# A graph convolution on one core: the one-hot matrix becomes the stationary operand, over groups of 512 edges

## The chip, the core and the metric

The kernel runs on one core of a Trainium2 chip. Its engines are TensorE (PE, with its weight loads as PEld), VectorE (DVE), ScalarE (ACT), GpSimd (POOL) and SyncE (SP), each with its own queue of instructions; semaphores tie them together. The metric is the device time of one execution in microseconds (us). Lower is better.

## The reference

12500 nodes with 128 features `x` (32 scalars and 32 vectors of 3), 412500 edges from `src` to `dst`, sorted by `dst`. Each edge has 4 attributes and 8 radial inputs. Cut to what matters:

```python
f0 = x0 @ W1_0e / sqrt(32);  f1 = einsum('nui,uw->nwi', x1, W1_1o) / sqrt(32)
e0, e1 = feat0[edge_src], feat1[edge_src]          # gather: 1 scalar and 3 vector parts, 32 wide
ea0, ea1 = edge_attr[:, :1], edge_attr[:, 1:4]
h = gelu(edge_scalar_attr @ W_mlp1 / sqrt(8));  h = gelu(h @ W_mlp2 / sqrt(64))
w00, w01, w10, w11 = h @ Wp_00, h @ Wp_01, h @ Wp_10, h @ Wp_11
out0_a = w00 * e0 * ea0
out0_b = w11 * sum(e1 * ea1[:, None, :], -1) / sqrt(3)
out1_a = (w01 * e0)[:, :, None] * ea1[:, None, :]
out1_b = w10[:, :, None] * e1 * ea0[:, :, None]
n0, n1 = segment_sum(mid0, edge_dst), segment_sum(mid1, edge_dst)    # mid: the outs, joined
y = cos * self + sin * (n @ W2) / sqrt(64)
x = layernorm(x + y)
```

All numbers are float32, but for the indices.

## The kernel before

`acc` holds the 12500 nodes as columns of 128 features and stays in SBUF. The program has three stages.

The first makes a table of features in HBM, from which edges are gathered later. Twenty-five batches of 4 x 125 nodes are loaded (SP, `load_x`, L274), transposed (PE L564), copied to `acc` (ACT L446), multiplied with `wfeat` (PE L591), copied (DVE L812) and stored by SP in 6 pieces (`store_table`, L287). Beside it DVE reduces the destinations of each group of 256 edges to their smallest number (L803, L804), POOL subtracts it (L383). Then all source indices and offsets are transposed by PE (L578) into `src_all` and `rel_all`, the attributes (L625) into `ea_all`, and the initial sums are made (L604, copied at L799). A flag tells whether all destinations of a group lie within a window of 16 nodes; here this holds for every group, and the `Else` branches don't run.

The second is the loop over 202 blocks of 2048 edges, which are 8 groups of 256. Block 0, the blocks 1 to 200 as 50 rounds of four, and block 201 are written out separately. The last block starts early enough to be full, and its doubled edges are left out. Per block:

- POOL gathers 16 tiles of 128 rows with an indirect DMA each (L388), in four chunks of 4 tiles, into one of 4 slots of `gath`. It waits for the block's indices in `idx` (L407), which ACT copies out of `src_all` (L450) in its step, three blocks ahead.
- SP loads the radial inputs `e8` (L343), one load for each block.
- PE transposes them (L642); ACT copies them (L484); layer 1 is 8 products of 128 columns (L650), ACT applies the activation (L472); layer 2 is 2 products of 512 columns (L656), ACT applies the activation (L478). All this is done for block b+1 in step b.
- `radial` (PE L666): 8 products of 256 columns make the four weights of every edge, in 4 chunks of one PSUM bank each.
- `multiply` (DVE L875, L878): for each chunk, radial weights (PSUM) times gathered rows (SBUF), into `prod`.
- `select` (DVE L862, L867): offsets are compared with 0 to 15 (`sel01`), then the one-hot matrix is multiplied with each of the 4 attributes: `sel`, 128 x 1024 for a block.
- `segment_sum` (PE L682): for each group, `prod` is the stationary operand (128 x 128) and `sel` the moving one (16 or 48 columns), 32 products per block. The result `z_ps` has features as rows.
- ACT copies the sums (`copy_sums`, L488), PE applies the second weights (`convolve`, L691, 4 products), DVE adds 8 windows of 16 columns into `acc` (`add_windows`, L900).

PE's order in a step is written out by hand (`step`, L696): each chunk's `radial`, then a part of the next block's layers, then the segment sum of two chunks earlier. DVE's step takes the four chunks in order, with `select` for the next block ahead of chunk 2, and the windows of the block before at the end. A float32 product shows up as two MATMUL records in the profile.

The third stage transposes the sums back (L763), normalises (DVE L964, L967, ACT L545, L550) and stores (L357).

Of the kernel before, what the change touches and what calls it, by code (L numbers as in the profile page):

```python
# [7 lines left out]
INT32 = mybir.dt.int32  # L8
# [9 lines left out]
NODE_P = 125  # L18
# [11 lines left out]
GROUP = 256  # L30
# [10 lines left out]
WINDOW = 16  # L41
EA_SLOTS = 8
SLOTS = 4
QUADS = (BLOCKS - 2) // SLOTS
assert BLOCKS == 2 + SLOTS * QUADS
# [14 lines left out]
def build_program(nc, x, src, dst, ea4, ea8, W1_0e, W1_1o, W_mlp1, W_mlp2, Wp, W2_0e, W2_1o, out):  # L60
    ctx = ExitStack()
    with ctx:
# [7 lines left out]
        base_dram = nc.dram_tensor("group_bases", [ROWS, 128], INT32, kind="Internal").ap()  # L70


        acc = sb("acc", [128, NODES + WINDOW])
        ea_all = sb("ea_all", [128, ALL_GROUPS * 2 * 4])
        rel_all = sb("rel_all", [128, ALL_GROUPS * 2], BF16)
        src_all = sb("src_all", [128, (BLOCKS + 2) * TILES], INT16)
        gath = sb("gath", [128, SLOTS, TILES, FEAT])
        idx = sb("idx", [128, SLOTS, TILES], INT32)
        e8 = sb("e8", [128, SLOTS, 128])
        e8T = sb("e8T", [128, 128])  # L80
        zsb = sb("zsb", [128, GROUPS * 4 * WINDOW])
        ident = sb("ident", [128, 128])
        iota_i = sb("iota_i", [128, WINDOW], INT32)
        iota_w = sb("iota_w", [128, WINDOW], BF16)
# [3 lines left out]
        wfeat = sb("wfeat", [128, 128])  # L88
        winit = sb("winit", [128, 128])
        conv = sb("conv", [128, 4, 128])  # L90
        base_f = sb("base_f", [128, ROWS])
        relmax = sb("relmax", [128, ROWS + 1])
        base13 = sb("base13", [ROWS, 128], INT32)
        base_row = sb("base_row", [1, ROWS * 128], INT32)
        flag_i = sb("flag_i", [1, 8], INT32)
        stats = sb("stats", [128, 4, NORM, 6])
# [4 lines left out]

        work = sb("work", [128, 9216])
        prod = work[:, 0:4096].rearrange("p (c t f) -> p c t f", c=CHUNKS, t=CT)
        sel = work[:, 4096:6144].rearrange("p (b t k w) -> p b t k w", b=2, t=TILES, k=4)
        h1 = work[:, 6144:7168].rearrange("p (h n) -> p h n", h=2)
        h2 = work[:, 7168:9216].rearrange("p (b e a) -> p b e a", b=2, a=8)
        ea_rows = work[:, 0:EA_SLOTS * 1024].rearrange("p (b e) -> p b e", b=EA_SLOTS)

        dst_rows = work[:, 2048:2048 + ROWS * 256].rearrange("p (c e) -> p c e", c=ROWS)
        src_rows = work[:, 2048 + ROWS * 256:2048 + 2 * ROWS * 256].rearrange("p (c e) -> p c e", c=ROWS)  # L110
        assert 2 * ROWS * 256 + 2048 <= 9216
        wself_raw = zsb[:, 0:128]
        x_rows = ea_all[0:NODE_P, 0:NODE_J * FEAT].rearrange("p (j d) -> p j d", d=FEAT)
        feat_rows = gath[0:NODE_P, :, :, :].rearrange("p s t f -> p (s t) f")[:, 0:PIECE_SLOTS * PIECE, :]\
            .rearrange("p (b j) f -> p b j f", b=PIECE_SLOTS)
        sel01 = sb("sel01", [128, TILES, WINDOW])
        conv_stage = sb("conv_stage", [128, 4, 128])

        diag = work[:, 4096:5120].rearrange("p (t k n) -> p t k n", t=2, k=4)
        gen_z = work[:, 3072:4096].rearrange("p (t k n) -> p t k n", t=2, k=4)  # L120

# [4 lines left out]
        z_ps = bank[6]  # L126
        t_ps = bank[0][:, 0:128]
        y_ps = bank[7][:, 0:128]

# [4 lines left out]
        s_dst = sem("dst_in")  # L134
        s_src0 = sem("first_src_in")
        s_src = sem("src_in")
        s_ea = [sem(f"ea_in{i}") for i in range(EA_SLOTS)]
        s_eaz = sem("ea_tail_zeroed")
# [6 lines left out]
        s_iota = sem("iota_ready")  # L145
        s_prep = sem("vector_chain")
        s_wnode = sem("node_weights_ready")
        s_xt = sem("x_transposed")
# [858 lines left out]
```

## Time and profile before

| | |
|---|---|
| median of 3 timed runs | 4366.4 us (4364.33 to 4367.3) |
| the profiled execution's own span | 6104.2 us |
| PE busy in it | 4593.2 us, 75% |
| PEld busy | 4019.8 us, 66% |
| POOL busy | 3171.7 us, 52% |
| DVE busy | 1755.8 us, 29% |
| ACT busy | 976.0 us, 16% |
| mean granted clock of TensorE | 0.707 |
| DMA | 254.36 MB, 42 GB/s on average |

The profiled execution is a single one, taken by the hardware profiler, and here it is much longer than the timed ones. Busy time counts an engine's own instructions; waiting, branching and issuing by its queue are not in it. PE's products are pipelined and their ends are modelled. The granted clock is a share of 2.4 GHz, and each moment has one of two levels, 1.0 or 0.5; a mean between them is a share of time.

### The profile page before, as it was taken

The page shows a single profiled execution, that of the slowest core. Times are in us where ns is not written, and L with a number is a line of the kernel's source. Part 1 is how long each engine was busy: PE and PEld are TensorE (multiplying, and loading weights), DVE is VectorE, ACT ScalarE, POOL GpSimd, SP SyncE. Part 2 cuts the span into 40 slices and gives each one's busy share as a digit, 9 for nine tenths or more (in the row PEclk, how much of TensorE's full clock was granted, in tenths as well). Part 3 has the DMA queues.
Part 4 walks back from the last instruction along what each step waited for, and adds up shares of the span by engine and source line. Part 5 has one row for each costly group of instructions (what it writes and reads, how often), then busy time and mean ns, then how long its engine had stood idle before and what let it go on. Part 6 is the DMA issues. An engine that isn't in the chain of part 4 may idle for free.

```text
span 6104.2 us, 62448 instructions
## 1 busy us (share of the span) xinstructions
PE 4593.2 (75%) x22626; PEld 4019.8 (66%) x22626; DVE 1755.8 (29%) x4788; ACT 976.0 (16%) x1595; POOL 3171.7 (52%) x3267
## 2 busy tenths in 40 slices
PE   5677777777777777777777777777777777777776
PEld 4466666667666666666666666667666666666665
DVE  2222223322332232222322223222222222233224
ACT  2211111111111111111111111111111111111113
POOL 3455555555655555555555455455555555555541
PEclk7767667776777677666766677676767767677667
DMA  4111111111111111111111111111111111111111
GB/s 149 48 37 37 37 37 40 42 42 37 43 39 42 37 40 37 38 38 37 40 37 38 35 39 41 33 40 40 38 39 40 37 37 37 40 38 42 39 29 52
DMA packets 142062, 254.36 MB, mean 42 GB/s; under 512 B 57365, under 2 KB 86467, under 8 KB 140538
## 3 DMA queue, kind: packets, MB, share of 16 engines
q0 software_dynamic: 103616, 211.52, 13.6%
q1 hardware_dynamic: 36726, 42.38, 2.0%
q10 hardware_dynamic: 1696, 0.18, 0.0%
q8 instruction: 11, 0.18, 0.0%
q14 instruction: 13, 0.11, 0.0%
HBM read 241.05 MB, written 12.81 MB: 42 GB/s over the span
## 4 chain that ended last, share of the span: by engine, by line
PE 63%; issue 20%; another core or an unknown queue 11%; ACT 3%; DMA 1%; SPq 0%; DVE 0%; ACTq 0%; DVEq 0%; POOL 0%; POOLq 0%
PE bank L682 27%; PE bank L666 14%; PE bank L650 11%; PE bank L656 7%; PE bank L691 3%; ACT work L478 2%; DMA ea_all<-in_x 1%; ACT ea_all L550 1%; ACT e8T L484 0%; SPq L281 0%; PE bank L642 0%; ACT ea_all L467 0%; PE bank L591 0%; PE bank L604 0%
## 5 line engine op out<-in xcount | busy, mean ns | idle before, releaser
L388 POOL DMA_INDIRECT gath<-feature_table,idx x3224 | 3148.9, 977 | 2759.2 <-ACT idx L450 1792.5
L682 PEld LDWEIGHTS bank<-work 128*128 128x128 f32 x12928 | 2150.1, 251 | 609.2 <-issue 544.0
L682 PE MATMUL bank<-work 128*128 128x16 f32 (+1 forms) x12928 | 2091.7, 312 | 306.4 <-issue 305.6
L650 PE MATMUL bank<-e8T,w1bd 128*128 128x128 f32 x3232 | 727.1, 393 | 1048.3 <-ACT e8T L484 526.9
L650 PEld LDWEIGHTS bank<-e8T,w1bd 128*128 128x128 f32 x3232 | 676.0, 297 | 1156.3 <-ACT e8T L484 564.8
L875 DVE TENSOR_TENSOR work<-bank,gath 128x256 f32<-128x256 f32 x808 | 342.7, 424 | 3589.4 <-remote 2297.5
L666 PE MATMUL bank<-wpbd,work 128*128 128x256 f32 x3232 | 1187.8, 504 | 1.5 <-issue 0.8
L878 DVE TENSOR_TENSOR work<-bank,gath 128x384 f32<-128x384 f32 x1616 | 818.0, 548 | 0.0
L666 PEld LDWEIGHTS bank<-wpbd,work 128*128 128x128 f32 x3232 | 742.7, 254 | 88.1 <-issue 1.8
L478 ACT ACTIVATE work<-bank 128x512 f32<-128x512 f32 x404 | 447.3, 1108 | 1343.9 <-PE bank L656 867.6
L656 PE MATMUL bank<-work,w2bd 128*128 128x512 f32 x808 | 565.0, 791 | 0.0
L472 ACT ACTIVATE work<-bank 128x512 f32<-128x512 f32 x404 | 237.3, 597 | 2011.9 <-remote 1411.5
L900 DVE TENSOR_TENSOR acc<-acc,bank 128x16 f32 x1616 | 276.0, 171 | 203.3 <-issue 16.3
L691 PE MATMUL bank<-zsb,conv 128*128 128x128 f32 x1616 | 283.8, 330 | 0.7 <-ACT zsb L488 0.7
L484 ACT COPY e8T<-bank 128x128 f32<-128x128 f32 x202 | 53.8, 266 | 1266.3 <-remote 1170.7
L867 DVE TENSOR_TENSOR work<-sel,ea_all 128x1024 f32<-128x1024 f32 x202 | 247.6, 1226 | 29.5
L691 PEld LDWEIGHTS bank<-zsb,conv 128*128 128x128 f32 x1616 | 249.5, 235 | 0.8 <-ACT zsb L488 0.8
L656 PEld LDWEIGHTS bank<-work,w2bd 128*128 128x128 f32 x808 | 210.0, 260 | 45.9 <-ACT work L472 0.5
L862 DVE TENSOR_TENSOR sel<-rel_all,iota_w 128x256 f32<-128x256 bf16 x202 | 85.8, 425 | 315.9 <-PE bank L682 314.1
L488 ACT COPY zsb<-bank 128x512 f32<-128x512 f32 x202 | 118.5, 587 | 302.2 <-PE bank L682 302.2
L642 PE MATMUL bank<-ident,e 128*128 128x128 f32 x202 | 59.1, 293 | 2.6 <-issue 2.2
L625 PEld LDWEIGHTS bank<-ident,work 128*128 128x128 f32 (+1 forms) x104 | 15.4, 201 | 63.9 <-issue 62.4
(70 smaller groups left out, 569.3 us busy)
## 6 DMA issues: line engine op xcount, KB each, us to landing
gath<-feature_table,idx POOLq DMA_INDIRECT x3224
e<-in_edge_attr SPq DMA_DIRECT2D x202, 64.0 KB
work<-in_edge_attr SPq DMA_DIRECT2D x12, 512.0 KB
ea_all<-in_x SPq DMA_DIRECT2D x4, 1250.0 KB
feature_table<-gath SPq DMA_DIRECT2D x4, 1250.0 KB
out<-ea_all SPq DMA_DIRECT2D x4, 1250.0 KB
work<-in_dst SPq DMA_DIRECT2D x1, 1536.0 KB
work<-in_src SPq DMA_DIRECT2D x1, 1408.0 KB
```

Source lines behind the costliest of these rows:

```text
L388: pool.indirect_dma_start(out=gath[:, s, t, :], out_offset=None, in_=table[:, :], in_offset=bass.IndirectOffsetOnAxis(ap=idx[:, s, t:t + 1 ...
L472: act.activation(h1[:, h, :], hid_ps[h][:, :], ACT.Gelu_apprx_tanh, scale=1.0 / math.sqrt(RADIAL)).then_inc(s_h1[h], 1)
L478: act.activation(h2[:, m % 2, :, 4 * h:4 * (h + 1)].rearrange("p e a -> p a e"), hid_ps[h][:, :].rearrange("p (a e) -> p a e", a=4), ACT.G ...
L650: last = pe.matmul(hid_ps[h][:, 128 * (a % 4):128 * (a % 4 + 1)], w1bd[:, a, :], e8T[:, :], start=True, stop=True)
L656: pe.matmul(hid_ps[h][:, :], w2bd[:, :], h1[:, h, :], start=True, stop=True).then_inc(s_h2p[h], 1)
L666: last = pe.matmul(wgt_ps[c][:, 256 * r:256 * (r + 1)], h2[:, m % 2, 16 * g:16 * (g + 1), :].rearrange("p e a -> p (e a)"), wpbd[:, :], st ...
L682: last = pe.matmul(z_ps[:, o:o + n * WINDOW], prod[:, c, 2 * r + e, 128 * half:128 * (half + 1)], sel[:, m % 2, 2 * g + e, half:half + n, ...
L691: last = pe.matmul(y_ps, conv[:, k, :], zsb[:, :].rearrange("p (g k w) -> p g k w", g=GROUPS, k=4)[:, :, k, :], start=(k == 0), stop=(k == 3))
L867: dve.tensor_tensor(sel[:, m % 2], sel01[:, :, :].unsqueeze(2).to_broadcast([128, TILES, 4, WINDOW]), attr.unsqueeze(3).to_broadcast([128, ...
L875: dve.tensor_tensor(o[:, :, :, 0, :], w[:, :, :, 0, :], f[:, :, 0, :].unsqueeze(2).to_broadcast([128, n, 2, MUL]), ALU.mult)
L878: last = dve.tensor_tensor(o[:, :, h, 1:4, :], w[:, :, h, 1, :].unsqueeze(2).to_broadcast([128, n, 3, MUL]), f[:, :, 1:4, :], ALU.mult)
L900: dve.tensor_tensor(acc[:, at], acc[:, at], y_ps[:, WINDOW * g:WINDOW * (g + 1)], ALU.add)\
```

## The change

- **Groups and windows.** A group has 512 edges (`GROUP`), a window 32 nodes (`WINDOW`); a block has 4 groups. An edge's place in a tile changes (`tile_of`): partition p holds edges 4p to 4p+3 of each group.
- **Streaming.** Sources, destinations and attributes aren't transposed ahead of the loop any more. SP loads them in the loop, two blocks at a time, into rings of 8 blocks (`src_t`, `dst_t`, `ea_t`), with 16, 16 and 64 bytes in a piece; the radial inputs come two blocks at a time too. The first 8 blocks are loaded between the table's stores. POOL gathers with indices straight from `src_t`, and waits for the products of the block four before.
- **Segment sum.** The one-hot `sel` (128 x 32, without attributes) is the stationary operand, `prod` the moving one with 256 columns: 16 products per block, the four groups on four 32-partition strips of `z_ps`. The sums are then transposed (2 products), copied, and multiplied with second weights by 2 products.
- **Attributes in the products.** DVE forms `dots` (three products of vector part and attribute), `dot1`, `dot`, then in each chunk `parts` (2 instructions that read PSUM), `dotted` (1, reads PSUM) and `wide` (3, all in SBUF).
- **Layers.** `e8` is transposed for four blocks at once, ACT copies 512 columns, layer 1 is 2 products of 512 columns per block, and the layers run four blocks ahead of `radial`.
- **First stage.** `init` runs within the batches. The groups' smallest destinations are reduced by DVE from `dst_rows`, and spread to all partitions by a product with ones (`base_bc`). The last block's 8 gathers that were skipped are issued, with its doubled edges' attributes zero.

```diff
-GROUP = 256
+GROUP = 512
-WINDOW = 16
+WINDOW = 32
...
@@ SP, first stage
             load_x(6)
+            for i in range(PAIR_SLOTS):
+                load_radial(2 * i, 2, 2 * i * BLOCK)
             store_table(2)
+            for i in range(PAIR_SLOTS):
+                load_src(2 * i, 2, 2 * i * BLOCK)
             store_table(3)
-            sp.dma_start(src_rows.bitcast(INT32)[:, 0, :], src_v[0:128, :]).then_inc(s_src0, 16)
+            for i in range(PAIR_SLOTS):
+                load_dst(2 * i, 2, 2 * i * BLOCK)
+                load_attributes(2 * i, 2, 2 * i * BLOCK)
...
             for n in range(4, PIECES):
                 store_table(n)
...
@@ SP, loop
-                with sp.Fori(1, QUADS) as n:
-                    for s in range(SLOTS):
-                        sp.wait_ge(s_tr, n * SLOTS + (s - SLOTS + 1))
-                        sp.dma_start(e8[:, s, :], e8_block((n * SLOTS + s) * BLOCK)).then_inc(s_e8[s], 16)
+                with sp.Fori(1, ROUNDS) as n:
+                    for i in range(PAIR_SLOTS):
+                        sp.wait_ge(s_prod[CHUNKS - 1], n * RING + (2 * i - RING + 2))
+                        load_src(2 * i, 2, n * (RING * BLOCK) + 2 * i * BLOCK)
+                        load_dst(2 * i, 2, n * (RING * BLOCK) + 2 * i * BLOCK)
+                        load_attributes(2 * i, 2, n * (RING * BLOCK) + 2 * i * BLOCK)
+                        sp.wait_ge(s_tr, n * 2 + (i // 2 - 1))
+                        load_radial(2 * i, 2, n * (RING * BLOCK) + 2 * i * BLOCK)
...
@@ POOL, loop
-                        pool.wait_ge(s_idx, n * SLOTS + (s + 1))
+                        pool.wait_ge(s_src[s % RING // 2], n * 16 + (16 + 16 * (s // RING)))
+                        pool.wait_ge(s_prod[CHUNKS - 1], n * RING + (s - SLOTS + 1))
                         pool.sem_inc(s_round, 1)
-                        for c in range(CHUNKS):
-                            gather(s, c)
+                        gather(s % SLOTS, s % RING)
...
@@ PE
+            def layer1(m, h):
+                pe.matmul(hid_ps[h][:, :], w1bd[:, 2 * (m % SUPER) + h, :], e8T[:, :], start=True, stop=True)\
+                    .then_inc(s_h1p[h], 1)
...
+                for par in range(2):
+                    for g in range(GROUPS):
+                        t = 2 * g + par
+                        last = pe.matmul(z_ps[32 * g:32 * (g + 1), :], sel[:, s % 2, 2 * t + eh, :],
+                                         prod[:, 2 * eh + g // 2, t % CT, :],
+                                         start=(eh == 0 and par == 0), stop=(eh == 1 and par == 1))
...
@@ DVE
+            def offsets(b, s):
+                dve.tensor_tensor(rel[:, :].rearrange("q (g e) -> q g e", e=4),
+                                  dst_t[:, s % RING, :].rearrange("q (g e) -> q g e", e=4),
+                                  base_bc[:, bass.ds(b * GROUPS, GROUPS)].unsqueeze(2).to_broadcast([128, GROUPS, 4]),
+                                  ALU.subtract).then_inc(s_rel, 1)
...
+            def dot_terms(rows, attr):
+                dve.tensor_tensor(dots[:, :, :, :], rows.rearrange("q t (s u) -> q t s u", s=4)[:, :, 1:4, :],
+                                  attr[:, :, 1:4].unsqueeze(3).to_broadcast([128, TILES, 3, MUL]), ALU.mult).then_inc(s_dots, 1)
...
+            def wide(c, rows, attr):
+                f = chunk_of(rows, c).rearrange("q t (s u) -> q t s u", s=4)
+                at = chunk_of(attr, c)
+                o = prod[:, c].rearrange("q t (h s u) -> q t h s u", h=2, s=4)
+                dve.tensor_tensor(o[:, :, 0, 0, :], prod_a[:, c % 2, :, 0, :],
+                                  at[:, :, 0:1].to_broadcast([128, CT, MUL]), ALU.mult)
+                dve.tensor_tensor(o[:, :, 1, 1:4, :], prod_a[:, c % 2, :, 1, :].unsqueeze(2).to_broadcast([128, CT, 3, MUL]),
+                                  at[:, :, 1:4].unsqueeze(3).to_broadcast([128, CT, 3, MUL]), ALU.mult)
+                return dve.tensor_tensor(o[:, :, 0, 1:4, :],
+                                         prod_b[:, c % 2].unsqueeze(2).to_broadcast([128, CT, 3, MUL]),
+                                         f[:, :, 1:4, :], ALU.mult)
```

## Rows read from the trace of the kernel before

**Rows 1.** The page: busy time of each engine; TensorE's granted clock in tenths, 40 slices.
```profile
PE 4593.2 (75%) x22626; PEld 4019.8 (66%) x22626; DVE 1755.8 (29%) x4788; ACT 976.0 (16%) x1595; POOL 3171.7 (52%) x3267
PEclk7767667776777677666766677676767767677667
```

**Rows 2.** Stretches: from:to, length, busy us (count) by engine, clock, DMA share, GB/s.
```profile
244.93:259.98 15.05, 15.05 (x111) 13.68 (x111) 7.57 (x18) 4.36 (x7) 5.01 (x5) 1.00 0.08 23
...
253.75:5982.00 5728.25, 4375.02 (x21521) 3838.13 (x21519) 1631.81 (x4343) 857.56 (x1381) 3086.41 (x3159) 0.70 0.15 38
```

**Rows 3.** Groups by shape: tile, shapes, count | busy us, mean ns | idle before, releaser.
```profile
L388 POOL DMA_INDIRECT gath<-feature_table,idx x3224 | 3148.9, 977 | 2759.2 <-ACT idx L450 1792.5 <-issue 966.8
...
L867 DVE TENSOR_TENSOR work<-sel,ea_all 128x1024 f32<-128x1024 f32 x202 | 247.6, 1226 | 29.5
...
L862 DVE TENSOR_TENSOR sel<-rel_all,iota_w 128x256 f32<-128x256 bf16 x202 | 85.8, 425 | 315.9 <-PE bank L682 314.1 <-issue 1.7
```

**Rows 4.** POOL's timeline: start us, length us, instruction, idle before and releaser.
```profile
111.12 1.07 POOL L388 DMA_INDIRECT gath<-feature_table,idx  x1 [36.31 <-issue]
...
253.75 1.28 POOL L388 DMA_INDIRECT gath<-feature_table,idx  x1 [61.88 <-ACT idx L450]
255.33 0.95 POOL L388 DMA_INDIRECT gath<-feature_table,idx  x1 [0.30 <-issue]
...
5982.01 0.96 POOL L388 DMA_INDIRECT gath<-feature_table,idx  x1 [0.30 <-issue]
```

**Rows 5.** The chain of waits from 5980 us on, in pieces: start, length, what.
```profile
5992.36 0.86 PE bank L656 x2
...
5995.89 0.87 PE bank L666 x4
5997.62 1.72 PE bank L682 x16
...
6030.16 2.05 PE bank L691 x8
```

**Rows 6.** Waits: who waited for whom, total us, times, longest us.
```profile
DVE work L875 <- remote: 2297.5, 291, 13.8
POOL gath L388 <- ACT idx L450: 1792.5, 198, 61.9
```

**Rows 7.** Timelines of VectorE and POOL where `select` meets a gather.
```profile
5947.80 1.23 DVE L867 TENSOR_TENSOR work<-sel,ea_all 128x1024 f32<-128x1024 f32 x1
...
5948.07 1.79 POOL L388 DMA_INDIRECT gath<-feature_table,idx  x1 [14.10 <-ACT idx L450]
...
252.97 1.23 DVE L867 TENSOR_TENSOR work<-sel,ea_all 128x1024 f32<-128x1024 f32 x1
...
5973.17 0.96 POOL L388 DMA_INDIRECT gath<-feature_table,idx  x1 [4.39 <-ACT idx L450]
5973.27 1.23 DVE L867 TENSOR_TENSOR work<-sel,ea_all 128x1024 f32<-128x1024 f32 x1
```

**Rows 8.** The timeline where products that read PSUM run beside a gather.
```profile
5974.41 0.42 DVE L875 TENSOR_TENSOR work<-bank,gath 128x256 f32<-128x256 f32 x1
5974.44 0.96 POOL L388 DMA_INDIRECT gath<-feature_table,idx  x1 [0.30 <-issue]
...
5974.75 1.01 DVE L878 TENSOR_TENSOR work<-bank,gath 128x384 f32<-128x384 f32 x2
```

**Rows 9.** SP's queue in the first stage: start us, length us, DMA issues.
```profile
11.55 12.90 SPq L281 DMA_DIRECT2D work<-in_dst  x1
...
63.81 19.82 SPq L287 DMA_DIRECT2D feature_table<-gath  x2
...
90.89 4.35 SPq L287 DMA_DIRECT2D feature_table<-gath  x2
...
95.78 11.04 SPq L281 DMA_DIRECT2D work<-in_src  x1
...
107.21 0.83 SPq L316 DMA_DIRECT2D work<-in_edge_attr  x2
```

More of the change, by code:

```diff
@@ L223, in build_program @@
         WEIGHTS_FROM = 3
[L224 to L232 removed]
+        OFFSETS_FROM = 8
         def norm_tiles(n):
@@ L491, in step, with copy_transposed @@
+            def copy_transposed(b):
+                act.wait_ge(s_ztp, b + 1)
+                act.copy(ztsb[:, :, :].rearrange("q h n -> q (h n)"), zt_ps).then_inc(s_zt, 1)
+            def step(b, s, k, first=False, last=False):
                 if not last:
[L492 to L494 removed]
+                    gelu1(b + SUPER, 0)
                 if not first:
                     copy_sums(b - 1)
[L497 to L499 removed]
@@ L521, in _ @@
-                step(BLOCKS - 1, BLOCKS - 1, last=True)
+                for m in range(SUPER):
+                    for h in range(2):
+                        gelu1(m, h)
+                    for h in range(2):
+                        gelu2(m, m, h)
+                copy_e8T(1)
+                step(0, 0, 0, first=True)
+                with act.Fori(0, ROUNDS) as n:
+                    for s in range(1, RING + 1):
+                        step(n * RING + s, s, n * 2 + (s // SUPER + 2))
+                step(BLOCKS - 1, 1, 0, last=True)
@@ new lines, in transpose_sums, with convolve, step @@
+                for h in range(2):
+                    last = pe.transpose(zt_ps[:, 128 * h:128 * (h + 1)], zsb[:, 128 * h:128 * (h + 1)], ident[:, :])
+                last.then_inc(s_ztp, 1)
+            def convolve(b):
+                pe.wait_ge(s_zt, b + 1)
+                for h in range(2):
+                    last = pe.matmul(y_ps, conv[:, h, :], ztsb[:, h, :], start=(h == 0), stop=(h == 1))
+                last.then_inc(s_y, 1)
+            def step(b, s, k, round_, first=False, last=False):
+                m = s % SUPER
+                radial(b, s, 0, first)
+                radial(b, s, 1, first)
+                if not last:
+                    if m == 0:
+                        pe.wait_ge(s_e8T, k + 0)
+                    pe.wait_ge(s_h2[0], b + SUPER)
+                    layer1(m, 0)
+                if not first:
+                    segment_sum(b - 1, s - 1, 1)
+                radial(b, s, 2, first)
+                radial(b, s, 3, first)
+                if not last:
+                    pe.wait_ge(s_h2[1], b + SUPER)
+                    layer1(m, 1)
+                if not first:
+                    transpose_sums(b - 1)
+                if not last:
+                    layer2(b + SUPER, 0)
+                segment_sum(b, s, 0, first)
+                if not last:
+                    layer2(b + SUPER, 1)
+                if not first:
+                    convolve(b - 1)
+                if m == SUPER - 1 and not last:
+                    pe.wait_ge(s_h2[0], b + (SUPER + 1))
+                    transpose_e8(s // SUPER % 2 * SUPER, round_)
```

833 lines of the change are left out of this document (392 added, 441 removed).

## The prediction

> **What bounds the kernel now.** I read the page first: TensorE is busy 75% of the span and POOL 52%, and the granted clock is 0.7 of full nearly everywhere [rows 1]. The span is 6104.2 us, but the median of the timed runs is 4366.4 us, so the profiled execution is 1.40 times as long as the timed ones, and its waits can't be carried over as they stand. So I ask of each engine how long one block of 2048 edges (202 of them) takes when nothing holds it up.
>
> TensorE: with all operands there, one block took 15.05 us at clock 1.00, with no idle time [rows 2]. At 0.70, the loop's mean [rows 2], this is 21.5 us; the profiled loop takes (5982 - 254) / 197.5 = 29.0 us per block.
>
> POOL: 16 gathers per block, mostly 0.96 us busy (the mean of 977 ns has the waits below in it) and 0.30 us idle [rows 3, 4]: 16 x 1.26 = 20.2 us per block. Nothing in it depends on TensorE's clock.
>
> Check against the timed run: gather 65 starts at 253.75 us (after 61.88 us of idleness, behind an index copy) [rows 4]. After the last gather (5982.01) come 122 us; the last conv is at 6030.16 [rows 5], 48 us or three blocks later, and two of these, 30 us, are backlog that a run bound by POOL doesn't have: about 92 are left. (4366.4 - 254 - 92) / 197.5 blocks = 20.4 us. POOL's own number is 20.2, so I take it that **the timed loop is bound by POOL's issue of gathers**; TensorE fits in at 15 to 20. The waits of the profile (POOL for index copies 1792.5 us, VectorE for releases that the profile can't place 2297.5 us [rows 6]) belong to an execution with a slower TensorE side.
>
> **A gather can be held up by VectorE.** L867 multiplies two SBUF operands, 1.23 us. In the loop the gather that meets it takes 1.27 to 1.28 us in place of 0.96, as at 253.75 [rows 4]; at 5948.07 one began 0.27 us after L867 (5947.80) and took 1.79 [rows 7]. Both end 0.83 us after L867 ends: 5949.03 to 5949.86, and 254.20 to 255.03. So the gather waits for the VectorE instruction that is running, then needs 0.83 us. A gather that began 0.10 us ahead of L867 took 0.96, and L867 its usual 1.23 (the last two of [rows 7]): VectorE isn't held in return. Products that read PSUM (L875, L878) don't do it: a gather beside one takes 0.96 [rows 8].
>
> **The change, part by part.**
>
> TensorE: radial 8 products of 256 columns stay. Layer 1 goes from 8 products of 128 columns to 2 of 512, priced as layer 2, 0.86 for one [rows 5]: 1.7 us at full clock. Segment sums: 32 products in 4 groups of 1.72 us [rows 5] become 16 with 256 moving columns; two radial products take 0.87 [rows 5], so 16 take 7.0 if they run one by one (lower bound 1.7 if the four that write different 32-partition strips overlap; no row shows it). Conv and transposes 1.0 to 0.7. Sum 3.5 + 1.7 + 1.7 + 7.0 + 0.7 = 14.6, against 15.05. It was not the bound, so worth 0.
>
> ScalarE: no index copy, smaller sum copies. Idle anyway, 0.
>
> VectorE: per block about 8850 elements per partition in 33 instructions, against 5500 in 22. By L862 (256: 425 ns) and L867 (1024: 1226 ns) [rows 3] an instruction costs 1.04 ns per element and 0.16 us, of which 0.08 overlap the next: 9.2 + 2.7, with waits some 14 us, under POOL's 20. The last block adds this whole pass behind the last gather in place of one chunk of 1.4 us, less the shorter rest: +7 us.
>
> What counts is which instructions read two SBUF tensors. Before: L862 and L867. After: the dot terms (1536 elements), two additions and the selection (512 each), the offsets (16), and three `wide` instructions in each of four chunks (128, 384, 384): 17 per block. A gather that arrives at random finds one of length d with chance d/P and waits d/2, so a block loses 16 x (sum of d squared) / 2P. With d = 1.04 n + 0.08: 1.68, three of 0.61, eight of 0.48, four of 0.21, 0.10; squares 5.97; 16 x 2.99 / 22 = 2.17 us. Before: 1.23 and 0.43, 16 x 0.84 / 20.2 = 0.67. Net **+1.5 us per block, 303 us in all**. Bounds: 0 (gathers settle into the gaps) and +2.9 (a gather has to let a whole run of such instructions pass, some 1.4 us each).
>
> POOL: 16 gathers as before; it now waits for products instead of an index copy, with four slots ahead, so not in the steady loop. The last block's 8 skipped gathers come back: +10 us. The idle 61.88 us before gather 65 go: block 0 is finished (landing, then 14 us of VectorE) long before 64 gathers (81 us) have been issued, as no index or attribute transposes stand between. **-62 us.**
>
> Prologue: the first gather starts at 111.12 us, 20 us behind the last two table stores, issued from 90.89 [rows 9]. SP now has, ahead of them, 4 radial loads, 4 of sources, 8 of destinations and attributes; the last 12 have 1024 pieces each of 16 or 64 bytes. SP was blocked 12.90 us behind a load of 1536 pieces and 11.04 us behind 1408 [rows 9], 8.4 and 7.8 ns a piece. At this price the sources take 33 us after the store at 63.81 (20 us of it were idle) and the other eight 66, so the first gather comes 72 us later. Where a queue isn't full an issue takes 0.4 us (two in 0.83) [rows 9], then 0 later. I take half: +35. All later blocks pass this queue too: 3 x 1024 pieces per two blocks are 26 us of SP in 43, enough room, and loads run several blocks ahead. The inits move into the batches; TensorE's and VectorE's share there is covered by the transfers of x.
>
> **Sum.** 4366 - 62 + 35 + 10 + 7 + 303 = 4659, say 4660 us, 6.7% slower than the median. The same as stages: first gather at 146, 202 blocks of 21.8 to 21.9, 97 behind. Against the profiled 6104.2 us this sum can't be made term by term, since there the 29 us blocks are TensorE's; in the changed kernel's profile I expect blocks of 21 to 23 us as well, since its TensorE issues half the instructions.
>
> The Trainium skill bears on this in "SBUF — State Buffer", § Who interferes with whom: a VectorE instruction with two SBUF inputs contends with a GpSimd instruction that reads SBUF, and whoever issues first has the port for the whole instruction; but it also reports a probe in which `tensor_tensor` didn't stall descriptor generation. By the first sentence, the gather that reads its index column is held, as in [rows 7]; by exclusion in both directions VectorE would be held as well, which the last two of [rows 7] speak against; by the probe no gather is held. What each gives is below.
>
> **Rivals.**
> - *The waits cost nothing* (gathers fall into gaps, or overlap what they lose). For: each chunk has instructions that read PSUM in between. Against: [rows 7]. Then 4366 - 62 + 35 + 10 + 7 = 4356 us, 4321 to 4393 with the bounds of the prologue. Chance 0.14, split over all three signs. The probe's result is this case.
> - *TensorE bound the timed loop after all, and POOL is quicker without a profile.* For: clock 0.70 in the trace, and 15.05 us at a mean clock of 0.74 is also 20.4. Against: POOL's number fits unaided. A block then scales with TensorE's work, 14.6 / 15.05 x 20.4 = 19.8, so 146 + 202 x 19.8 + 97 = 4243 us; if the strips overlap, POOL's 16 x 0.96 + 2.2 = 17.6 is left, 3800 us. I give it 4200, as no row shows the overlap. Faster. Chance 0.16.
> - *Slower by another bound.* TensorE idles a third of each block; if the clock then stays at half, 14.6 becomes 29.2 us and 202 blocks 5900; it decides from a clock of 14.6 / 21.8 = 0.67 on, just under the 0.70 seen. Or gathers and two-operand instructions exclude each other both ways: 16 x 0.96 + 10 = 25.4, so 5370 us. Chance 0.12.
> - *The forecast:* 0.58, on its own 4480 to 4900.
>
> **Chances.** Range 4180 to 4960 us: it takes in the first rival, most of the forecast's bounds (+2.9 a block gives 4945) and the nearer end of the second. A difference of 0.2% is about what a measurement of this kernel can tell. Faster by more: 0.16 + 0.05 + 0.02 of the forecast's own edge = 0.23. Same 0.06. Slower 0.71.
>
> **What would show it.** Right: gathers' mean well above 0.96 us, those above it ending 0.83 us after a VectorE instruction with two SBUF operands; POOL without idle gaps beyond 0.30 us; no gap at gather 65; first gather between 111 and 183 us. Wrong: gathers at 0.96 throughout; or POOL waiting for products, with TensorE at half clock; or a block under 20 us, which would mean that POOL's 1.26 us was the profile's own.

## The result and the profile after

| | us |
|---|---|
| before, median of 4 runs | 4366.9 (4364.3 to 4367.6) |
| after, median of 4 runs | 4507.6 (4504.2 to 4508.3) |
| ratio | 1.0325, 95% interval 1.0310 to 1.0339: slower |
| profiled execution of after, its own span | 4502.4 |

Chips differ for this kernel: on some of them before takes 4360 us, on others 6117 or more (by its length the profile shown of before, 6104.2, is of the second kind), so the time of before on the same chip is given with the runs below.

The page of after: busy time by engine, the granted clock in 40 slices, the chain of work that ended last, and the costliest group, which answers to [rows 1] and the gathers of [rows 3].

```profile
PE 2636.5 (59%) x13221; PEld 1544.9 (34%) x13221; DVE 2475.8 (55%) x6961; ACT 914.6 (20%) x1417; POOL 3321.0 (74%) x3263
PEclk9777777787777777777777777777777777778776
POOL gath L399 73%; ACT big L539 1%; PE bank L573 0%; DMA big<-in_x 0%; SPq L285 0%; DMA feature_table<-gath 0%; SPq L293 0%; PE bank L560 0%; POOLq L415 0%; DMA wself_raw<-in_L_gnn_W_1o 0%; SPq L289 0%; PE bank L553 0%; DVE top_f L784 0%; DVE base_f L782 0%; PE bank L581 0%
L399 POOL DMA_INDIRECT gath<-feature_table,src_t x3232 | 3310.3, 1024 | 1095.7 <-issue 1095.7
```

POOL carries 73% of the chain that ends last, and its 1095.7 us of idle time are the 111.1 before the first gather and 0.305 between any two: it waits for nobody. So the time is (first gather) + (3232 gathers) + (what follows). The gathers alone, from the first to the last (POOL's timeline, as [rows 4]):

```profile
122.85 1.02 POOL L399 DMA_INDIRECT gath<-feature_table,src_t  x1 [111.11 <-issue]
...
4416.86 0.95 POOL L399 DMA_INDIRECT gath<-feature_table,src_t  x1 [0.30 <-issue]
```

(4416.86 - 122.85) / 3231 x 16 = 21.26 us per block, and 85.5 us follow the last. A block in which no gather were held would take 16 x (0.944 + 0.305) = 19.98. The other 1.28 us are two gathers in each block, the same two in every block: of a block's sixteen gathers the third is held 201 times and the eighth 201 times, no other ever. One block, VectorE and POOL (start, length, instruction):

```profile
2016.47 1.76 DVE L821 TENSOR_TENSOR dots<-gath,ea_t 128x1536 f32<-128x1536 f32 x1 [8.25 <-DMA gath<-feature_table,src_t]
2017.53 1.51 POOL L399 DMA_INDIRECT gath<-feature_table,src_t  x1 [0.30 <-issue]
...
2020.40 0.28 DVE L851 TENSOR_TENSOR big<-prod_a,ea_t 128x128 f32<-128x128 f32 x1
2020.60 0.94 POOL L399 DMA_INDIRECT gath<-feature_table,src_t  x1 [0.30 <-issue]
2020.61 0.58 DVE L853 TENSOR_TENSOR big<-prod_a,ea_t 128x384 f32<-128x384 f32 x1
...
2024.13 0.54 DVE L853 TENSOR_TENSOR big<-prod_a,ea_t 128x384 f32<-128x384 f32 x1
2024.34 1.61 POOL L399 DMA_INDIRECT gath<-feature_table,src_t  x1 [0.30 <-issue]
2024.60 0.54 DVE L855 TENSOR_TENSOR big<-prod_b,gath 128x384 f32<-128x384 f32 x1
```

The first held gather ends at 2019.04, 0.81 us after the dot terms (2018.23); the second at 2025.95, 0.81 after L855 (2025.14), not after L853 that was running when it began: here the product that followed without a gap held it too (the run below in which the dot terms read PSUM shows that this is no rule). The gather at 2020.60 began 0.08 us before the end of L851 and 0.01 us before L853, with L855 behind that, all of two SBUF inputs, and took its usual 0.94.

### The profile page after: what moved, and what is told of

The parts are those of the page before. It is cut to its first block, busy times and chain, and to the rows that moved or that the text cites. A ratio compares the mean times of both kernels' runs of the same rounds, so it can differ in the third digit from the quotient of the medians.

```text
span 4502.4 us, 45613 instructions
## 1 busy us (share of the span) xinstructions
PE 2636.5 (59%) x13221; PEld 1544.9 (34%) x13221; DVE 2475.8 (55%) x6961; ACT 914.6 (20%) x1417; POOL 3321.0 (74%) x3263
## 4 chain that ended last, share of the span: by engine, by line
POOL 73%; issue 22%; PE 1%; ACT 1%; DMA 1%; SPq 1%; DVE 1%; POOLq 0%; ACTq 0%; DVEq 0%
POOL gath L399 73%; ACT big L539 1%; PE bank L573 0%; DMA big<-in_x 0%; SPq L285 0%; DMA feature_table<-gath 0%; SPq L293 0%; PE bank L560 0%; POOLq L415 0%; DMA wself_raw<-in_L_gnn_W_1o 0%; SPq L289 0%; PE bank L553 0%; DVE top_f L784 0%; DVE base_f L782 0%; PE bank L581 0%
## 5 line engine op out<-in xcount | busy, mean ns | idle before, releaser
L399 POOL DMA_INDIRECT gath<-feature_table,src_t x3232 | 3310.3, 1024 | 1095.7 <-issue 1095.7
L630 PE MATMUL bank<-big,sel 128*32 128x256 f32 x6464 | 566.9, 480 | 1584.8 <-DVE big L855 1584.8
L615 PE MATMUL bank<-wpbd,big 128*128 128x256 f32 x3232 | 886.5, 422 | 0.3 <-ACT big L468 0.3
L468 ACT ACTIVATE big<-bank 128x512 f32<-128x512 f32 x410 | 443.1, 1082 | 2109.0 <-PE bank L604 2109.0
L615 PEld LDWEIGHTS bank<-wpbd,big 128*128 128x128 f32 x3232 | 661.2, 216 | 172.6 <-issue 84.8
L604 PE MATMUL bank<-h,w2bd 128*128 128x512 f32 x820 | 586.4, 806 | 0.0
L853 DVE TENSOR_TENSOR big<-prod_a,ea_t 128x384 f32<-128x384 f32 x804 | 444.1, 552 | 0.0
L855 DVE TENSOR_TENSOR big<-prod_b,gath 128x384 f32<-128x384 f32 x808 | 439.7, 544 | 0.0
L599 PE MATMUL bank<-e8T,w1bd 128*128 128x512 f32 x820 | 431.4, 609 | 1.5 <-ACT big L468 0.8
L840 DVE TENSOR_TENSOR prod_b<-bank,ea_t 128x128 f32<-128x128 f32 x804 | 222.1, 276 | 0.0
L851 DVE TENSOR_TENSOR big<-prod_a,ea_t 128x128 f32<-128x128 f32 x804 | 221.9, 276 | 0.0
L599 PEld LDWEIGHTS bank<-e8T,w1bd 128*128 128x128 f32 x820 | 163.8, 201 | 31.9 <-ACT big L468 5.2
```

Source lines behind the costliest of these rows:

```text
L399: pool.indirect_dma_start(out=gath[:, s, n, :], out_offset=None, in_=table[:, :], in_offset=bass.IndirectOffsetOnAxis(ap=src_t[:, r, n:n + ...
L468: act.activation(h2[:, m // SUPER % 2, :, a // 4, :, a % 4], hid_ps[h][:, :].rearrange("q (b p) -> q b p", b=SUPER), ACT.Gelu_apprx_tanh, ...
L599: pe.matmul(hid_ps[h][:, :], w1bd[:, 2 * (m % SUPER) + h, :], e8T[:, :], start=True, stop=True)\
L604: pe.matmul(hid_ps[h][:, :], w2bd[:, :], h1[:, h, :], start=True, stop=True).then_inc(s_h2p[h], 1)
L615: last = pe.matmul(wgt_ps[c][:, 256 * r:256 * (r + 1)], h2[:, s // SUPER % 2, s % SUPER, eh, 32 * g:32 * (g + 1), :] .rearrange("q p j -> ...
L630: last = pe.matmul(z_ps[32 * g:32 * (g + 1), :], sel[:, s % 2, 2 * t + eh, :], prod[:, 2 * eh + g // 2, t % CT, :], start=(eh == 0 and par ...
```

## The experiments

**Theories.** *Phase*: VectorE's pass over a block starts when the block's 16th gather has landed, so gathers and VectorE operations meet in the same way in every block; a gather is held when its start falls into a run of two-SBUF operations, until the run's end. *Random arrivals*: the prediction's sum of squares. *TensorE*: it bounds before or after, or both.

### On chips where before takes 6117 us

Four runs on one such chip. The shift adds, after the wait for the gathers and one for the first weights:

```
+ for i, n in enumerate((256, 256)):
+     dve.tensor_copy(spare[:, i, 0:n], wgt_ps[0][:, 0:n])
  dot_terms(rows, attr)
```

> The changed kernel with two extra VectorE copies (PSUM to SBUF, 256 elements per partition each, some 0.65 us together, one SBUF side only, so that they hold no gather by themselves) ahead of the dot terms in each block: the same work of two-SBUF operations, only about 0.65 us later against the gathers. Phase theory (the pass starts at the landing of the block's last gather, so the same gathers meet the same VectorE operations in every block, and a gather whose start falls into a run of two-SBUF operations waits for the run's end): the two holds get longer with the shift, 21.9 instead of 21.27 us per block, total 4630 to 4660 us. Random-arrival theory (holds are drawn as the sum of squared durations over twice the period, as in my prediction): a shift changes nothing, 4500 to 4515 us. A theory that TensorE or VectorE bounds the loop: up to 0.65 us more per block as well, but then the gathers show idle behind the landing and not behind VectorE operations.

Measured: 5567.7 us, before 6115.6 beside it (median of 11 executions, 5994.7 to 6169.6 and a single one of 8780.0).

The layout and the copy of the attributes, then the operations that read it:

```
- zt_ps, y_ps = bank[7][:, 0:256], bank[7][:, 256:384]
+ zt_ps, y_ps = bank[6][:, 256:512], bank[5][:, 0:128]
+ attr_ps = bank[7][:, 384:448]     # copied once a block, after the last product
```

> Control for the next two: the changed kernel with its PSUM banks laid out anew (transposed sums beside the sums in bank 6, the convolution's output in the bank of the last chunk's weights, so that bank 7 is free for VectorE), which makes each block's convolution wait for VectorE's last product, plus one small VectorE copy per block of the next block's attributes into PSUM, read by nobody. All of it lies in VectorE's and TensorE's slack of about 8 us per block. Phase theory and random-arrival theory: 4507 us, within 0.5%, 21.3 us per block. If TensorE were near the bound: 0.5 to 1 us more per block, 4610 to 4710.

```
- dot_terms(rows, attr)
+ dot_terms(rows, attr_ps)
```

> The control with one operation changed: the dot terms (1.76 us, the longest operation with two SBUF inputs) take the attributes from PSUM, so they have one SBUF input. Phase theory: the first hold of 0.61 us goes, the gathers behind it start earlier by that, and then fall into the middle of the later products instead of near their ends; simulated from the trace's durations 22.5 us per block, 4700 to 4760 us: slower by taking a hold away. Random-arrival theory: about 1.1 us per block less (the dots carry most of the sum of squares), some 4290 to 4330 us. Hold not from the two SBUF inputs at all: 4507.

```
  rel, prod_b and the attributes of every wide() in bank 7
- dot1 = dots[0] + dots[1];  dot = dot1 + dots[2]
+ dve.tensor_reduce(dot, dots.rearrange("q t k u -> q t u k"), AXIS_X, ALU.add)
```

> The control with every VectorE operation of the loop that had two SBUF inputs (but the 16-element offsets) given one input from PSUM: attributes, relative offsets and the first-part products stand in PSUM, and the two adds over the dot terms become one reduction. Same result. If holds by two-SBUF operations are all that stands between 21.27 and 16 x 1.249 = 19.98 us per block: 4240 to 4260 us, and gathers show a mean near 0.94 us with none above 1.1. If the longer gathers come from anything else (transfers, descriptors, other SBUF traffic): 4507. If TensorE is the bound at about 20.4 us per block as one rival of the prediction has it for before: 4330 to 4370.

Measured: 5518.2, 5816.3 and 6072.8 us. All four expectations were set against 4366 us and can't be judged by these times. What can be read is the gathers: in the last one their mean is 0.946 us and none is above 1.1, so with no VectorE operation of two SBUF inputs no gather is held. But they now wait for products, and the products for TensorE. Timeline of the last one, a group of sum products and the copy that waits for it:

```profile
3007.06 1.07 PE L636 MATMUL bank<-big,sel 128*32 128x256 f32 x16
...
3019.34 0.37 ACT L476 COPY zsb<-bank 128x256 f32<-128x256 f32 x1 [11.57 <-remote]
```

Two stretches of it, with the columns of [rows 2]:

```profile
3010.00:3014.00 4.00, 0.92 (x3) 0.09 (x1) 2.90 (x10) 0.00 (x0) 3.08 (x4) 1.00 0.21 55
3014.00:3018.00 4.00, 0.00 (x0) 0.00 (x0) 0.00 (x0) 0.00 (x0) 3.09 (x4) 0.63 0.21 59
```

The release came 12 us after the products' recorded start and 8 us after the last product recorded before it: the first stretch, at full clock, has the rest of that one (to 3010.91), the second, at a mean clock of 0.63, has none. The profile of before is of this kind too, with its "releases that the profile can't place" [rows 6]. On another chip of this kind:

> The changed kernel unaltered, beside the runs of the kernel before on the same chip: on the chip of the first four runs the kernel before took 6116 us instead of 4366, with TensorE's semaphores up to 12 us behind its recorded work, so that nothing there could be set against the 4507 us. Every theory: 4500 to 4515 us where before takes 4366; where before takes about 6100, TensorE is the bound, and the changed kernel, with 42% fewer TensorE instructions, is the faster one: 5400 to 5600 us, as the control run in that state had 5518.

> Again the changed kernel with no VectorE operation of two SBUF inputs in the loop (but the 16-element offsets). Where before takes 4366 us: 4240 to 4260 if holds are all that stands between 21.27 and 19.98 us per block, with no gather above 1.1 us; 4507 if not; 4330 to 4370 if TensorE bounds at about 20.4 us. In the first look its gathers did lie at 0.946 us with none held, but TensorE was the bound. In that state again: 6070.

> Again the changed kernel with two VectorE copies of 256 elements ahead of the dot terms. Where before takes 4366 us: phase theory 4630 to 4660 us (21.9 us per block, same two gathers held, longer), random arrivals 4500 to 4515. In the other state: 5570.

Measured: after 5532.6 us against 6119.4 for before, ratio 0.904 (0.898 to 0.911); without two-SBUF operations 6049.6; with the short shift 5566.5. There the change makes the kernel faster by a tenth, as its expectation said, and taking the holds away makes the changed one slower by 9%. Why TensorE's releases are late on these chips, and why quicker gathers make it worse, I didn't find out; it stays open.

### TensorE taken out

The next kernels read only the upper halves of the operands in the loop's products, and keep all else, the transposes too:

```
+ def top(tile):
+     return tile.bitcast(BF16)[:, 1::2]
- pe.matmul(wgt_ps[c][...], h2[...], wpbd[:, :], ...)
+ pe.matmul(wgt_ps[c][...], top(h2[...]), top(wpbd[:, :]), ...)   # and so in every product of the loop
```

They ran on chips where before took 4361 and 4358 us.

> On both chips so far the kernel before took 6117 us, not the 4366 us of the recorded comparison, and VectorE and ScalarE waited up to 12 us for TensorE's semaphores behind its recorded products. This takes TensorE out of the question: the changed kernel with every matrix product of the loop reading only the upper halves of its float32 operands (as bfloat16, so the output has that precision and is not the reference's); everything else, all waits included, as it was. If the 4507 us of the recorded comparison are gathers plus the two held gathers per block and nothing of TensorE: 4480 to 4515 us here, 21.1 to 21.3 us per block, two gathers of 1.5 to 1.65 us in each block. If TensorE had a part in them: under 4450. If the slow state is not TensorE's: still 5530.

> The kernel before with the same edit (the loop's products in bfloat16, output of that precision). If before was bound by its gathers at 16 x 1.263 = 20.2 us per block plus one hold of 0.3 by its window selection in the recorded comparison: 4340 to 4370 us, and the ratio of the two light kernels repeats the recorded 1.0325 within 0.005. If TensorE bound it at 4366: under 4300. If something else is slow on this chip: far above 4366.

Measured: 4503.4 and 4351.1 us (before: 4361.2). The ratio of the two light kernels is 1.0350, the recorded one 1.0325. TensorE's busy time in the changed kernel falls from 2636.5 to 1265.4 us and the time by 4: TensorE has next to no part in the 4507. The light kernel before tells what the long profile of before couldn't. Its gathers by shape, and its timeline where one meets the selection:

```profile
L388 POOL DMA_INDIRECT gath<-feature_table,idx x3224 | 3178.2, 986 | 1018.4 <-issue 1018.4
```

```profile
3014.70 1.22 DVE L871 TENSOR_TENSOR work<-sel,ea_all 128x1024 f32<-128x1024 f32 x1
3015.33 1.42 POOL L388 DMA_INDIRECT gath<-feature_table,idx  x1 [0.30 <-issue]
```

The idle 1018.4 us are 36.0 before the first gather and 0.305 each: there is no gap before gather 65. One gather per block is held (the twelfth of the sixteen, in 197 of 199 cases), to 0.83 us after the selection's end, 0.50 us in the mean: 16 x (0.955 + 0.305) + 0.50 = 20.65 us per block, as its timeline has it.

> The light changed kernel with no VectorE operation of two SBUF inputs in the loop but the 16-element offsets (products in bfloat16, output of that precision). Theory of holds: 16 x 1.251 = 20.0 us per block, 4240 to 4260 us. Rival, the gathers are not held by these operations or something else takes the freed time: near 4500.

Measured: 4243.2 us. Its gathers, against 1024 ns in the changed kernel:

```profile
L401 POOL DMA_INDIRECT gath<-feature_table,src_t x3232 | 3050.9, 944 | 1095.2 <-issue 1095.2
```

The two-SBUF operations are the whole of the difference: 4503.4 - 4243.2 = 260 us, 1.29 per block.

```
  the window selection's relative numbers and single one-hots in PSUM
- sel01 = (rel_all == iota_w);     work = sel01 * ea_all      # both inputs in SBUF
+ sel01_ps = (rel_all == iota_ps); work = sel01_ps * ea_all   # iota_ps, sel01_ps in bank 7
```

> The light kernel before (products in bfloat16, output of that precision) with its window selection's numbers and single-group one-hots in PSUM, so that its VectorE has no operation of two SBUF inputs at any of its selections. It was 4351 us with a hold of 0.50 us per block. If that hold is all that its gathers pay: 20.15 us per block, 4240 to 4260 us. If before pays nothing for holds because something else fills the time: 4350.

Measured: 4249.1 us, the mean of a gather 954 ns, none held. Before paid 102 us for its one hold a block. Without holds on either side the change is worth 4249.1 - 4243.2 = 6 us, 0.14%. The two ran on different chips, on which before takes 4358.4 and 4361.2, so the 6 us by themselves are near what a comparison of two chips can tell; the terms of the two traces (first gather +11.5, eight gathers +10, tail +7, shorter gathers -34) give the same.

### Where the holds fall

> The light changed kernel with two extra VectorE copies of 256 elements ahead of the dot terms (products in bfloat16, output of that precision); they hold nothing themselves. Phase theory: the same two gathers held, each longer, 21.9 us per block, 4630 to 4660 us. Random arrivals, the sum of my prediction: a shift changes nothing, within 10 us of the light changed kernel.

Measured: 4651.6 us, 22.0 us per block. The same two gathers are held in each block; the first now starts just behind the start of the dot terms:

```profile
2015.20 0.76 DVE L887 COPY spare<-bank 128x256 f32<-128x256 f32 x2 [9.16 <-DMA gath<-feature_table,src_t]
2015.88 1.75 DVE L827 TENSOR_TENSOR dots<-gath,ea_t 128x1536 f32<-128x1536 f32 x1
2016.12 2.32 POOL L400 DMA_INDIRECT gath<-feature_table,src_t  x1 [0.30 <-issue]
```

VectorE idles 9 us a block, yet the copies, which put the dot terms off by 0.74 us, cost 0.73 us a block, on POOL.

```
+ the same with four copies: (256, 256, 256, 64)
```

> The light changed kernel with four extra VectorE copies ahead of the dot terms (256, 256, 256 and 64 elements, some 1.25 us; one SBUF side, products in bfloat16, output of that precision). The shorter shift of 0.7 us cost 0.73 us per block. Phase theory: at 1.25 us the pattern has moved on by one gather (16 gathers start every 1.25 us), the dots meet the next gather at the same place as without a shift, and the time falls back: 21.2 us per block, 4490 to 4510 us. A theory that later VectorE work simply costs what it is late: 1.25 us per block more, 4750 us. Random arrivals: 4503.

Measured: 4491.1 us, 21.20 us per block. The dot terms come 1.19 us later than without copies, 1.6 times the delay of the short shift, and its loss is gone:

```profile
2010.60 1.22 DVE L887 COPY spare<-bank 128x256 f32<-128x256 f32 x4 [7.93 <-DMA gath<-feature_table,src_t]
...
2011.49 0.94 POOL L400 DMA_INDIRECT gath<-feature_table,src_t  x1 [0.30 <-issue]
2011.73 1.75 DVE L827 TENSOR_TENSOR dots<-gath,ea_t 128x1536 f32<-128x1536 f32 x1
2012.74 1.56 POOL L400 DMA_INDIRECT gath<-feature_table,src_t  x1 [0.30 <-issue]
```

The gather at 2011.49 starts before the dot terms and is free; the next meets them in their second half. In the mean of all blocks the first gather that starts inside the dot terms does so 1.00 us behind their start without copies, 0.27 with the short shift and 1.06 with the long one: the long shift has moved the pattern on by one gather, as the phase theory had it. Random arrivals can't give 4503, 4652 and 4491 us for the same operations.

> The light changed kernel (products in bfloat16, output of that precision) with the bank layout of the second run and one operation changed: the dot terms take the attributes from PSUM, so that they no longer have two SBUF inputs and hold no gather. Phase theory: the gather behind them starts 0.6 us earlier, and so do the next, which then start inside the runs of products instead of between them; worked out with the trace's durations 22.5 us per block, 4720 to 4780 us, slower by removing a hold. Random arrivals: the dots carry over half of the sum of squares, about 1.1 us per block less, 4270 to 4330 us.

Measured: 4495.0 us: both numbers missed. The dots' hold is gone, and the gathers lose 1.16 us per block all the same, now at the additions and the later products. (The 1.16 is of the profiled execution, the quickest of the four at 4479.5; they spread up to 4500.0. And the bank layout with its added waits wasn't run alone in the light form.) The phase theory has the reason right (what one hold doesn't take the next ones do) and the size wrong. Its 22.5 us took every run of operations that follow without a gap to hold as one. One block of the trace:

```profile
2014.32 0.73 DVE L840 TENSOR_TENSOR dot<-dot,dots 128x512 f32<-128x512 f32 x1
2014.33 0.94 POOL L401 DMA_INDIRECT gath<-feature_table,src_t  x1 [0.30 <-issue]
...
2015.17 0.55 DVE L863 TENSOR_TENSOR big<-prod_a,ea_t 128x384 f32<-128x384 f32 x1
2015.57 0.97 POOL L401 DMA_INDIRECT gath<-feature_table,src_t  x1 [0.30 <-issue]
2015.64 0.55 DVE L865 TENSOR_TENSOR big<-prod_b,gath 128x384 f32<-128x384 f32 x1
2016.11 0.48 DVE L855 TENSOR_TENSOR big<-bank,dot 128x128 f32<-128x128 f32 x2
...
2016.71 0.55 DVE L863 TENSOR_TENSOR big<-prod_a,ea_t 128x384 f32<-128x384 f32 x1
2016.85 1.22 POOL L401 DMA_INDIRECT gath<-feature_table,src_t  x1 [0.30 <-issue]
2017.18 0.55 DVE L865 TENSOR_TENSOR big<-prod_b,gath 128x384 f32<-128x384 f32 x1
```

The first gather starts 0.01 us behind the start of the addition L840, and isn't held. The other two start inside L863 and end 0.81 to 0.82 us after its end (2015.72 to 2016.54, and 2017.26 to 2018.07), although L865 follows without a gap: the run doesn't hold them. The ten traces of the changed kernel and its variants that have such pairs of products show 1338 gathers that waited for the second product too, and all of these began 0.16 to 0.24 us behind the start of the first; 335 others, nine tenths of them begun earlier or later than that, were let go at the first one's end. Why that narrow place differs no run here tells. A few hundredths of a microsecond decide between nothing and half a microsecond, and the durations that I worked from aren't known that well; here, too, the held gathers aren't the same in each block (512 holds, at the fourth to the eighth gather).

### A kernel that beats both

Full precision, no two-SBUF operation in the loop but the offsets, and:

```
+ for n in range(4, PIECES): store_table(n)
  for i in range(PAIR_SLOTS):
      load_dst(...); load_attributes(...)
- for n in range(4, PIECES): store_table(n)
```

> The changed kernel in full precision with no VectorE operation of two SBUF inputs in the loop but the 16-element offsets, and with the last table stores issued ahead of the destination and attribute loads. Its light form was 4243 us. Where before takes 4361: 4225 to 4240 us, the first gather at 105 to 115 us instead of 122.8, loop at 19.98 us per block. If full-precision products make TensorE late at that pace: above 4300. On a chip where before takes 6117: 6050, with the first gather at 105 to 115 all the same.

Measured: 4238.9 us against 4358.4 for before, ratio 0.9726 (0.9710 to 0.9742), and 6.0% under the changed kernel's 4507.6. The loop is as expected, the first gather a microsecond later than I allowed (timeline, then the gathers by shape):

```profile
116.16 1.02 POOL L401 DMA_INDIRECT gath<-feature_table,src_t  x1 [104.41 <-issue]
```

```profile
L401 POOL DMA_INDIRECT gath<-feature_table,src_t x3232 | 3050.3, 944 | 1088.9 <-issue 1088.9
```

This holds for chips of the quicker kind. On the others the same kernel without the moved stores took 6050 us where the change as given took 5533.

> The kernel before in full precision, with its window selection's numbers and single-group one-hots in PSUM (no selection of two SBUF inputs). Its light form was 4249 us at 20.15 us per block. If TensorE has room at that pace on a chip where before takes 4360: 4250 to 4262 us, so that the change itself, with no holds on either side, is worth 10 to 20 us (4239 against this). If TensorE's 22.7 us of recorded products per block are near the bound: 4300 to 4360. On a chip where before takes 6117: near 6100, and nothing is told.

Measured: 6921.5 us, before 6520.9 on that chip, ratio 1.055 (1.044 to 1.066): on this kind of chip taking the hold away makes before slower too. By the expectation's last sentence this tells nothing of the question; that before without holds has room on TensorE in full precision is not shown.

## Why the prediction was right or wrong

**What bounds the kernel: right.** POOL's issue of gathers bounds before (20.65 us per block in the light form, which is 10 us short of the full one) and after (21.26). The rival that TensorE bound the timed loop is out: in the light forms over half of its busy time is gone (1357.5 us are left in before, 1265.4 in after), and the times fall by 10 and 4 us.

**That holds decide the sign: right, and not by the sum.** With all holds removed from both kernels (light forms) the difference is 6 us the other way.

**The size of the holds: wrong, the step that failed.** "A gather that arrives at random" gave 2.17 us per block for after and 0.67 for before, net 303 us. Measured 1.29 (260 us in all) and 0.50 (102 us), net 158 us. Gathers don't arrive at random: the pass that holds them is released by them. The evidence is the same two gathers in every block, and the shifts (4503, 4652, 4491 us). The sum had two slips beside this, which nearly cancel. The products take 0.54 and 0.28 us, not 0.48 and 0.21. And a held gather needs 0.82 us behind the operation where an unheld one takes 0.94 ([rows 7] had 0.83 against 0.96), so each wait costs 0.12 less than the sum took. With both put right, the lengths to be squared are 1.64, three of 0.56, eight of 0.42 and four of 0.16, their squares 5.14, and random arrivals give 16 x 5.14 / (2 x 21.26) = 1.9 us for after, and 0.5 for before in the same way (an estimate from these lengths): some 290 us net, still 130 too much. At best this is the mean over all phases: of the three measured, two give 1.2 and 1.3 and one 2.0 us. That it gives before's 0.50 is luck, as there too the same gather is held each time.

**The 61.9 us before gather 65: wrong.** I took off 62 us for a gap that stands in the profile of before [rows 4] (and again, with 62.1, in the last run above, on a chip of that kind) and not in the light form of before on a quicker chip. As the full form takes only 10 us more there, I take it that at most 10 us of the gap are in the timed 4366; no profile of the full form on such a chip shows it. I had said that the waits of that profile can't be carried over, and carried this one over. My own check could have told: with the gap it left 20.4 us per block, 0.2 above POOL's 20.2, where the holds that I reckoned for before were 0.67. Without it gather 65 starts at 192, and (4366.4 - 192 - 92) / 197.5 = 20.67, with the 0.5 of holds that was measured.

**A gather's own length: missed.** I let it stay at 0.96 and 0.30. Unheld it is 0.955 in before and 0.944 in after; by the periods of the two kernels without holds, (20.15 - 19.98) x 202 = 34 us that the change gives and the sum lacks. Why it is shorter no run here tells.

**The first gather: right in kind, size off.** +35 taken of 0 to 72; measured 122.85 - 111.12 = +11.7. SP's queue in the prologue of after, as [rows 9]:

```profile
48.15 22.96 SPq L297 DMA_DIRECT2D e<-in_edge_attr  x4
71.15 6.00 SPq L269 DMA_DIRECT2D feature_table<-gath  x1
77.19 15.03 SPq L285 DMA_DIRECT2D src_t<-in_src  x4
...
93.26 7.13 SPq L293 DMA_DIRECT2D ea_t<-in_edge_attr  x1
100.43 3.90 SPq L289 DMA_DIRECT2D dst_t<-in_dst  x1
104.37 0.58 SPq L293 DMA_DIRECT2D ea_t<-in_edge_attr  x1
...
108.60 0.72 SPq L269 DMA_DIRECT2D feature_table<-gath  x2
```

The four source loads took 15 us where 33 were priced, the eight behind them 14.6 where 66 were: two took 11.0 together, the others 0.6 each. I read the two as waits for a queue that was full; no row shows the queue. Moving the stores ahead of the eight brought 6.7 us (122.85 to 116.16), not 14.6, because the stores then took 9.4 us of SP's time at the same place.

**The last block: right.** +7 forecast; 77.3 us follow the last gather in the light kernel before, 83.5 in the light one after: +6. But the 97 of the stages came from the 92 that I had worked out of the long profile, and the changed kernel has 85.5.

**Together,** from the light kernel before to the light one after: holds +158, first gather +12, eight more gathers +10, tail +6, shorter gathers -34. That is +152, and 4503.4 - 4351.1 = 152. The forecast was +293: 145 too much in holds, 23 in the first gather, 1 in the tail, 34 for the shorter gathers, less the 62 of the gap, are 141 = 293 - 152. The recorded pair differs by 141: the full kernel before stands 10 us above its light form (4361.2 against 4351.1), and the full kernel after 4 above its own; what the 10 are is open.

**The rule of the Trainium skill** ("SBUF — State Buffer", § Who interferes with whom) weighed in the prediction: the rows here bear out its first sentence in one direction, a gather that starts inside a VectorE instruction of two SBUF inputs waits for that instruction's end (up to 1.4 us lost, with the short shift), unless it starts in about the first 0.02 us, or in the last 0.12 us, where the wait costs nothing. In the other direction an instruction that starts inside a gather, or just ahead of one, isn't held for it: VectorE lost 0.05 us in the rows above (0.73 for 0.68; 0.58 for 0.54 at 2020.61) and 0.08 at most in those traces. The probe in which `tensor_tensor` didn't stall descriptor generation doesn't describe these gathers: taking the second SBUF input away gave 260 us.

## What to carry to other kernels

Where GpSimd issues gathers back to back and bounds the loop, every VectorE operation beside them with two SBUF inputs can cost time although VectorE idles nearly half the span; put one input in PSUM where a bank is free, for all of them, as removing one alone moved the loss to the next. Where the holding engine starts its pass on a result of the held one (here VectorE on the 16th gather), don't reckon with random arrivals: lay the two timelines over each other from that start on, and take edges within some hundredths of a microsecond as open. Take no gap over from a profiled execution that isn't as long as the timed ones.

## What the hardware showed that I hadn't expected

- A gather waits for the operation in which it starts, and at one narrow place for the next one too: one that starts 0.21 us into L853 waits for L855 behind it (0.67 us where 0.33 of L853 were left), one that starts 0.14 or 0.40 us into the same product (L863 where the dot terms read PSUM) doesn't. At the junction of two such operations it is free, as at 2020.60.
- The four products that write different 32-partition strips run beside each other. Timeline of after: 8 products in 16 records, and the copy that waits for them starts 1.14 us after the first, where two radial products of the same 256 columns take 0.87 us [rows 5] and 8 one by one would take 3.5.

```profile
2028.42 1.07 PE L630 MATMUL bank<-big,sel 128*32 128x256 f32 x16
2029.56 0.37 ACT L474 COPY zsb<-bank 128x256 f32<-128x256 f32 x1 [0.43 <-PE bank L630]
```

- One and the same kernel takes 4361 or 6117 us (6521 on one) depending on the chip, or on its state at the time, which no run here separates, with TensorE's releases up to 12 us late, and the two kinds of chip put these kernels in opposite order.
